# Scatter-add in two column halves into two output tensors, with GpSimd's weight copies moved to VectorE and ScalarE

## What is computed

```python
ys = _geglu(xf @ Ws1 + bs1) @ Ws2 + bs2              # shared expert, every token
top_val, top_idx = jax.lax.top_k((xf @ Wr + br) / TAU, 2)
top_w = jax.nn.softmax(top_val, axis=-1)             # w: its one-hot sum over 12 experts
h = jnp.einsum('nd,edh->enh', xf, We1) + be1[:, None, :]
act = _geglu(h)                                      # a * gelu(g), 768 wide
yE = jnp.einsum('enh,ehd->end', act, We2) + be2[:, None, :]
yr = jnp.einsum('end,ne->nd', yE, w)
x = x + (ys + yr)
```

## Time and profile before

| | us |
|---|---|
| median of 3 runs | 805.79 |
| profiled execution, its own time | 806.17 |
| its span | 804.4 |
| PE busy (share of the span) | 783.6 (97%) |
| DVE busy | 575.9 (72%) |
| ACT busy | 294.3 (37%) |
| POOL busy | 405.4 (50%) |
| 75 indirect scatters on POOL (L504) | 120.6 |
| 75 indirect gathers on POOL (L496) | 75.1 |
| POOL's 75 copies of a weight block and 75 of the bias part | 30.4 and 42.8 |

### The profile page before, as it was taken

One profiled execution on the slowest core, in us unless ns is written; L12 is line 12 of the kernel. 1 busy time (PEld: TensorE's weight loads), 2 busy tenths in 40 slices (PEclk: granted clock), 3 DMA queues, 4 the chain that ended last, 5 costly groups with the idle time before them and its releaser, 6 DMA issues.

```text
span 804.4 us, 27682 instructions
## 1 busy us (share of the span) xinstructions
PE 783.6 (97%) x9379; PEld 658.2 (82%) x9380; DVE 575.9 (72%) x1350; ACT 294.3 (37%) x883; POOL 405.4 (50%) x511
## 2 busy tenths in 40 slices
PE   7999999999999999999999999999999999999994
PEld 6788888888888888777778888888888888888883
DVE  2999877777777777679884676666666666666661
ACT  1444444444444444542222333333333333333330
POOL 3133244444444444401012777777777777777762
PEclk9999999999999999999999999999999999999998
DMA  9553355555565554048734233223222322232222
GB/s 277 153 187 101 112 170 180 182 174 177 180 182 181 182 182 146 2 158 232 231 130 139 28 42 37 33 35 39 35 34 33 38 38 33 34 40 36 33 31 26
DMA packets 49325, 86.11 MB, mean 107 GB/s; under 512 B 7298, under 2 KB 27970, under 8 KB 49122
## 3 DMA queue, kind: packets, MB, share of 16 engines
q1 hardware_dynamic: 33778, 68.83, 27.2%
q0 software_dynamic: 13888, 15.13, 14.3%
q10 hardware_dynamic: 1584, 1.10, 0.5%
HBM read 68.48 MB, written 16.55 MB: 106 GB/s over the span
## 4 chain that ended last, share of the span: by engine, by line
PE 90%; DVE 5%; issue 2%; DMA 1%; SPq 0%; POOL 0%; ACT 0%; DVEq 0%
PE ps L1575 24%; PE ps L1562 13%; PE ps L1234 7%; PE ps L1473 6%; PE ps L1332 4%; PE ps L1556 4%; PE ps L1306 3%; PE ps L1250 3%; PE ps L1279 3%; PE ps L1462 3%; PE ps L1219 3%; PE ps L1543 2%; PE ps L1339 2%; PE ps L1292 2%; PE ps L1321 2%
## 5 line engine op out<-in xcount | busy, mean ns | idle before, releaser
L1575 PE MATMUL ps<-arena,stage 128*128 x900 | 206.6, 379 | 0.0
L1575 PEld LDWEIGHTS ps<-arena,stage 128*128 128x128 f32 x900 | 165.2, 190 | 19.5
L504 POOL DMA_INDIRECT out_dram<-stage,to_row x75 | 120.6, 1609 | 76.0 <-DVE stage L1143 71.3
L708 ACT ACTIVATE stage<-ps 128x384 f32<-128x384 f32 x150 | 65.4, 488 | 241.6 <-PE ps L1562 241.6
L1562 PE MATMUL ps<-token_rows,token_rows_T 64*128 64x128 f32 x1800 | 129.2, 272 | 0.0
L1562 PEld LDWEIGHTS ps<-token_rows,token_rows_T 64*128 64x128 f32 x1800 | 118.8, 188 | 1.7
L496 POOL DMA_INDIRECT token_rows<-gated_rows,from_row x75 | 75.1, 1001 | 61.6 <-DVE to_row L1022 38.9
L1117 DVE COPY token_rows<-ps 128x128 f32<-128x128 f32 x75 | 21.9, 292 | 111.8 <-PE ps L1544 111.8
L408 POOL TENSOR_TENSOR arena<-arena 128x256 f32<-128x256 f32 x32 | 23.4, 732 | 139.3 <-DVE arena L832 132.3
L1127 DVE TENSOR_TENSOR stage<-ps,stage 128x384 f32<-128x384 f32 x150 | 76.0, 549 | 1.8 <-ACT stage L708 1.8
L795 DVE TENSOR_REDUCE arena<-ps 128x8 f32<-128x512 f32 x64 | 43.9, 686 | 42.4 <-PE ps L1270 42.0
(11 more groups left out here) (173 smaller groups left out, 1473.8 us busy)
## 6 DMA issues: line engine op xcount, KB each, us to landing
stage<-in_we_dram SPq DMA_DIRECT2D x36, 512.0 KB, 4.7
arena<-in_cond_w_dram SPq DMA_DIRECT2D x64, 256.0 KB, 2.8
arena<-in_we_dram SPq DMA_DIRECT2D x12, 768.0 KB, 6.0
arena<-in_x_both_dram SPq DMA_DIRECT2D x31, 256.0 KB, 2.7
arena<-in_L_cond_bias_dram SPq DMA_DIRECT2D x64, 64.0 KB, 2.9
out_dram<-arena SPq DMA_DIRECT2D x32, 128.0 KB, 2.7
be_bc<-in_be_rows_dram SPq DMA_DIRECT2D x13, 192.0 KB, 3.4
gated_rows<-token_rows POOLq DMA_DIRECT2D x2, 1152.0 KB, 11.6
```

What stands on the lines that cost most here:

```text
L504: pool.indirect_dma_start(out_rows, bass.IndirectOffsetOnAxis(to_row[:, t:t + 1], 0), y_sb[t % YR], None, compute_op=ALU.add).then_inc(d_a ...
L708: nc.scalar.activation(g_sb[hf].rearrange("p (j n) -> p j n", n=P), first_out[1][:, :, hf, :], ACT.Gelu).then_inc(g_ok, 1)
L1575: last = mm(ps[:, 4 + s % 2, 0:D], actT_sb[s % 2][:, hf, j * P:(j + 1) * P], arena[:, ds(e * E2 + (NJ * hf + j) * D, D)], start=(hf == 0 a ...
```

## The change

Each scatter is made in two halves of 128 columns, into two output tensors of 128 columns, which are put side by side on the host. Each half has a semaphore of its own and waits for the same half of the tile before. The stores of the shared expert and the padding rows are split in the same way: two DMAs each for one. POOL's `copy_last` is gone, and its waits with it. DVE copies block 2 besides block 1, with a load of `expert_of` for each; ACT copies the bias part besides block 0, in a new function `tile_weights`.

```diff
-        d_add = sem("d_add")
+        d_add = [sem(f"d_add{h}") for h in range(2)]
...
                 sp.wait_ge(comb_ok, n + 1)
-                sp.dma_start(out_rows[ds(n * P, P), :], x2res[:, ds(n * D, D)]).then_inc(d_out, 16)
+                for h in range(2):
+                    sp.dma_start(out_half[h][ds(n * P, P), :], x2res[:, ds(n * D + h * P, P)]).then_inc(d_out, 16)
...
             def add_rows(t, s):
                 pool.wait_ge(y_ok, t + 1)
-                if t > 0:
-                    pool.wait_ge(d_add, 16 * t)
-                pool.wait_ge(d_dummy, 16)
-                pool.indirect_dma_start(out_rows,
-                                        bass.IndirectOffsetOnAxis(to_row[:, t:t + 1], 0),
-                                        y_sb[t % YR], None, compute_op=ALU.add).then_inc(d_add, 16)
-
-            def copy_last(t):
-                copy_first(pool, nc.gpsimd.tensor_copy, t, t, 2)
-                e = pool.value_load(expert_of[0:1, ds(t, 1)], min_val=0, max_val=NE - 1)
-                nc.gpsimd.tensor_copy(w1bx[t % 2].bitcast(bf16), w1b[:, ds(e * (NJ * P), NJ * P)]).then_inc(w1bx_ok, 1)
+                pool.wait_ge(d_dummy, 32)
+                for h in range(2):
+                    part = slice(h * P, (h + 1) * P)
+                    if t > 0:
+                        pool.wait_ge(d_add[h], 16 * t)
+                    pool.indirect_dma_start(out_half[h],
+                                            bass.IndirectOffsetOnAxis(to_row[:, t:t + 1], 0),
+                                            y_sb[t % YR][:, part], None, compute_op=ALU.add).then_inc(d_add[h], 16)
...
-            pool.wait_ge(r_done, 1)
-            pool.wait_ge(shx_ok, TOK // U)
-            pool.wait_ge(l_cut, 4 * (NE + 1))
-            for t in range(2):
-                copy_last(t)
...
             for t in range(NS):
-                if t + 2 < NS:
-                    pool.wait_ge(h_ps, t + 1)
-                    copy_last(t + 2)
                 if t > 0:
                     add_rows(t - 1, (t - 1) % RING)
...
+            def tile_weights(t, s):
+                copy_first(act, copy, t, s, 0)
+                e = act.value_load(expert_of[0:1, ds(t, 1)], min_val=0, max_val=NE - 1)
+                copy(w1bx[s % 2].bitcast(bf16), w1b[:, ds(e * (NJ * P), NJ * P)]).then_inc(w1bx_ok, 1)
...
                     if s + 2 < left:
-                        copy_first(act, copy, t + 2, s, 0)
+                        tile_weights(t + 2, s)
                         widen(t + 2, (s + 2) % RING, 16 * q + (16 if s + 2 < RING else 32))
...
                 if not (isinstance(t, int) and t < YR):
-                    dve.wait_ge(d_add, 16 * t - 16 * (YR - 1))
+                    for h in range(2):
+                        dve.wait_ge(d_add[h], 16 * t - 16 * (YR - 1))
...
                     if not last or s + 2 < NS % RING:
-                        copy_first(dve, V.tensor_copy, t + 2, s, 1)
+                        for j in (1, 2):
+                            copy_first(dve, V.tensor_copy, t + 2, s, j)
                     gate_bias(t, s)
```

More of the change, by code:

```diff
@@ L40, with adaln_attn_moe @@
 ALI = P + 4 * S
-def adaln_attn_moe(nc, args, out):
+def adaln_attn_moe(nc, args, out_half):
     f32, bf16, i32, u32 = mybir.dt.float32, mybir.dt.bfloat16, mybir.dt.int32, mybir.dt.uint32
@@ L47, in adaln_attn_moe @@
     a = args
-    out_rows = out
     ctx = ExitStack()
@@ L380, in _ @@
                     store_out(2 * u + v, d_out_low)
-            sp.wait_ge(d_out_low, 16 * low_tiles)
+            sp.wait_ge(d_out_low, 32 * low_tiles)
             for e in overlap:
@@ L454, in _ @@
             pool.dma_start(gated_rows[PAD_ROW:PAD_ROW + P, :], zero_row).then_inc(d_zero, 16)
-            pool.dma_start(out_rows[TOK:TOK + P, :], zero_out).then_inc(d_dummy, 16)
+            for h in range(2):
+                pool.dma_start(out_half[h][TOK:TOK + P, :], zero_out[:, 0:P]).then_inc(d_dummy, 16)
             def tile_steps(i, odd, last=False):
@@ L516, in _ @@
                 load_rows(s, s)
-            pool.wait_ge(r_done, 1)
-            pool.wait_ge(shx_ok, TOK // U)
-            pool.wait_ge(l_cut, 4 * (NE + 1))
-            for t in range(2):
-                copy_last(t)
-            pool.wait_ge(d_out_low, 16 * low_tiles)
-            pool.wait_ge(d_out_high, 16 * (NT - low_tiles))
+            pool.wait_ge(d_out_low, 32 * low_tiles)
+            pool.wait_ge(d_out_high, 32 * (NT - low_tiles))
             for t in range(NS):
-                if t + 2 < NS:
-                    pool.wait_ge(h_ps, t + 1)
-                    copy_last(t + 2)
                 if t > 0:
@@ L532, in _ @@
             add_rows(NS - 1, (NS - 1) % RING)
-            pool.wait_ge(d_add, 16 * NS)
+            for h in range(2):
+                pool.wait_ge(d_add[h], 16 * NS)
         @block.scalar
@@ L722, in _ @@
             act.wait_ge(shx_ok, TOK // U)
+            act.wait_ge(l_cut, 4 * (NE + 1))
             for t in range(2):
@@ L725, in _ @@
             for t in range(2):
-                copy_first(act, copy, t, t, 0)
+                tile_weights(t, t)
             shared_gelu(TOK // U - 1)
@@ L1064, in _ @@
             dve.wait_ge(d_zero, 16)
-            dve.wait_ge(d_dummy, 16)
+            dve.wait_ge(d_dummy, 32)
             dve.wait_ge(l_cut, 4 * (NE + 1))
@@ L1166, in _ @@
             for t in range(2):
-                copy_first(dve, V.tensor_copy, t, t, 1)
+                for j in (1, 2):
+                    copy_first(dve, V.tensor_copy, t, t, j)
             for v in range(2):
@@ L1705 @@
                                     kind="ExternalInput").ap()
-    out = nc.dram_tensor("out_0_dram", (TOK + P, D), mybir.dt.float32, kind="ExternalOutput").ap()
-    adaln_attn_moe(nc, args, out)
+    out_half = [nc.dram_tensor(f"out_{h}_dram", (TOK + P, P), mybir.dt.float32, kind="ExternalOutput").ap()
+                for h in range(2)]
+    adaln_attn_moe(nc, args, out_half)
     r = run_bass_kernel_spmd(nc, [arrays], core_ids=[0])
-    return r.results[0]["out_0_dram"][:TOK].reshape(B, S, D)
+    return np.concatenate([r.results[0][f"out_{h}_dram"][:TOK] for h in range(2)], axis=1).reshape(B, S, D)
```

## The result

The changed kernel takes 829.93 us, median of 4 runs (829.41 to 830.89), against 805.9 before: a ratio of 1.0301, 95% interval 1.0288 to 1.0314. The profiled execution took 829.45 us.

A forecast was written before the change was run, and what follows sets the result against it. PE at 4.73 us a tile bounds the kernel before; the change makes POOL the bound at 5.21. From 445.85, 69 x 5.21 plus the tail gives span 834.8, 836 against the median; range 808 to 860.

The forecast's parts named there:

- the chain of landings: Waits between scatters: landing 3.8 us plus 0.7 to the next start allows one per 4.5 us, under PE's 4.73.
- Half a scatter at full price: On POOL, each half scatter costs 1.61 us like a whole, as the rows stay 128 and both halves still add.
- Three gaps of 0.307: On POOL, one gap for each of three indirect DMAs a tile, 0.92 us together.
- busy time alone: POOL's period without the gaps, 4.22 us, which would fit under PE's 4.73.
- 0.07 a tile for the port: POOL loses 0.07 us a tile to DVE's copies and bias multiply, which get through mostly in the gaps.
- The way from POOL to PE: A slow POOL reaches PE through DVE's y, which waits for landings; PE idle 0.4 to 0.5 us a tile.
- The five last steps: Tail without gathers: the chain of landings sets 4.2 us a step, with a half landing after 3.5.
- Copies on VectorE and ScalarE, stores in halves, PE's clock: Load of the moved copies on DVE and ACT, 32 more store issues, and a lower PE clock: no cost expected.
- A price by bytes: Rival: POOL's half scatter costs 1.19 us, PE keeps 4.73, no loss, time 805; chance 0.16.
- The port as a dear term: Rival: port sharing between DVE and POOL makes 5.5 to over 6 us a tile, 890 at 6.0; chance 0.10.
- The Trainium skill's fit: DMA time as 2.0 us + bytes / 436e3: a half lands only 0.15 sooner, the sum 1 us higher.
- The argument from transfers under 64 KB: Against the scatter split: the skill's rule that transfers under 64 KB mostly pay overhead; no size given.

The follow-up runs named there:

- e1: Kernel before with only the copies moved from POOL to DVE and ACT, the scatter left whole: 805.71 us against 805.89.
- e7: e1 with one more gather a tile, into a buffer that nothing reads: 806.73 us.
- e4: The changed kernel with half scatters that write instead of adding: 803.21 us, one execution.
- e10: e1 with its whole scatter writing instead of adding: 801.93 us, one execution.
- e3: The changed kernel with each half scatter cut to the first 64 of its 128 rows: 809.06 us, a single execution.
- e8: e1 with two more gathers a tile, into buffers that nothing reads: 879.04 us.
- e6: The changed kernel with block 2 copied by ScalarE and not by VectorE: 829.66 us against the change's 829.93.
- e2: The changed kernel with the scatter split but the copies left on POOL: 883.62 us, ratio 1.0963 to the kernel before.

## Why the prediction was right, and where it was off

- **What bounds the kernel before**: PE at 4.73, with the chain of landings at 4.5 and POOL's three instructions under it. Right; e1 and e7 change POOL's load in both directions and the time stays. That loosening the chain buys nothing is right too: e4 brings it from 4.5 down to 2.9 us, and the pace stays 4.73.
- **Half a scatter at full price**: taken 1.61, measured 1.58. The reason given, that the adding and not the bytes makes the price, is shown by e4 and e10. The other half of it, "since the number of rows stays 128", hardly counts: 64 rows cost 1.43 (e3).
- **Three gaps of 0.307**: right (0.305), and shown by e8 to be time that POOL can't use: without them it would have kept PE's pace. The 4.22 of "busy time alone" would have said that the change is free.
- **0.07 a tile for the port**: wrong. The step that failed reads: "a DVE copy from SBUF to SBUF waits for POOL's indirect DMA. POOL will be in one for nearly all of the period, so the two copies and the bias multiply get through mostly in the gaps". They don't need the gaps, as DVE's and POOL's timelines show together:

```profile
603.04 1.02 POOL L497 DMA_INDIRECT token_rows<-gated_rows,from_row  x1 [0.30 <-issue]
...
603.58 0.28 DVE L269 COPY token_rows_T<-w_merged 128x256 f32 x1
...
604.37 1.58 POOL L507 DMA_INDIRECT out_dram<-stage,to_row  x1 [0.31 <-issue]
...
604.87 0.68 DVE L1131 TENSOR_SCALAR token_rows_T<-be_bc,token_rows 128x256 f32 x1 [0.48 <-issue]
```

The copy lies wholly inside a gather and takes 0.28, as when POOL does nothing. The multiply inside the scatter is held up, to 605.55, 0.40 before the scatter's end and not after it. POOL did not lose 0.07 a tile but about 1 us in all 75: 24 of the 150 halves took longer than 1.58, by 1.1 us together. Taking one of the three operations away (e6) changed nothing. The step rested on one row beside a POOL copy, in which a VectorE copy that begins 0.34 into a gather is held to its end. In e1, where no POOL copy follows the gather, copies that begin up to 0.53 into it take about 0.29.
- **The way from POOL to PE**: wrong as well, at no cost to the sum. The prediction has PE "waiting for DVE's y, which itself waits for landings". The runs show the gathers in that place: ACT waits for gathered rows in 35 of 40 tiles, 65.8 us in 200, and DVE's sum for no landing. PE's tile is 0.36 us longer, 5.09 for 4.73, near the "PE idle 0.4 to 0.5 a tile" of the forecast, though the busy column doesn't show it.
- **The size.** The span came to 827.1 where my sum had 834.8. Of the 7.7 us, 8.1 come from the period, 69 x 5.21 = 359.5 against 351.3: 0.07 for the port, 0.06 for two halves at 1.58 and not 1.61, less 0.02 for a longer gather. The five last steps took 4.02 and not 4.2 (0.9), the last landing 3.3 and not 3.5 (0.2). Against that the stage began 0.3 later, and the program's close behind the last landing took 4.4 and not 3.1. Without the charge for the port the sum would have come to 830.0. The longer close was not foreseen; by luck it hides 1.3 us of what the sum had too much.
- **Copies on VectorE and ScalarE, stores in halves, PE's clock**: no cost foreseen. None was found for the copies (e1) and the clock (1.00 in the stretch). No run splits the stores alone; at most they hold the 0.3 us by which the first scatter came later.
- **Rivals.** A price by bytes is out (e10). The port as a dear term is out by the 1.1 us above, VectorE's load by e1 and e6.
- The Trainium skill's fit, DMA: Bandwidth & Descriptors, "Anatomy of one DMA", would let a half land 0.15 sooner; the landing came 0.5 sooner (3.3 for 3.8), so here the measurement stands. For scatters that don't add it is near the fit, 2.2 for 2.4 (e4, e10). The same section calls descriptor generation small; POOL's instruction for one indirect DMA takes 1.0 to 1.6 us here, and is the bound.
- The argument from transfers under 64 KB doesn't reach this split: a half holds 64 KB, not less, and in e4 the same halves, not adding, cost nothing.

## What to carry to other kernels

Count an indirect DMA on POOL by its instruction time plus the gap of 0.3 us behind it, and compare that sum, not the busy time, with the pace of the engine that bounds. Splitting an adding scatter halves neither: POOL pays the price again for each piece. Before loosening a chain of waits, compare its step (landing plus 0.7) with the pace it would have to beat. Where one queue holds scatters and gathers, look for the effect of slow scatters in late gathers too; here it was there, and not in the y buffers.

## What the runs showed beyond that

- POOL's time for an indirect DMA of 128 rows is 0.94 to 1.02 us for a gather or a plain scatter, whether the rows have 288, 512 or 1024 bytes, and mostly 1.55 to 1.62 for one that adds; with 64 rows, 1.43 (e3). The adding costs landing time too: 3.3 against 2.2 for a half (e4).
- DVE's copy and bias multiply are held up only by a part of POOL's indirect DMA. In the changed kernel's trace, operations that begin 0.50 to 0.81 into an adding scatter end 0.40 before its end; those that begin in the first 0.4 run freely; in a gather those that begin up to 0.59 are free, and from 0.61 to 0.78 they end 0.09 after it. In the kernel before, one that began 0.34 into a gather was held to its end. There a POOL copy is next in the queue, here and in e1 another indirect DMA; e1 points to that copy as the cause, and no run tries it alone.
- The holding up goes the other way too. The Trainium skill, SBUF — State Buffer, "SBUF: two separate sides", gives the shared port pair to whichever of the two starts first, and has a GpSimd DMA wait for DVE. Of the 24 longer scatters, 19 had one of these DVE operations still running 0.13 to 0.24 into them, and ended 1.43 to 1.46 after it; the longest, in which a DVE copy had begun 0.05 before it, took 1.69 for 1.58. Both agree with the page, save that neither holds for the whole instruction.
- The gap ahead of an indirect DMA depends on what stands before it: 0.30 behind another indirect DMA, 0.16 behind a copy (e2).
- The close of the program after the last landing took 4.4 us in the changed kernel and 3.1 before. The difference lies in POOL's last instruction, a DRAIN: 2.68 us before and 2.69 in e1, 3.87 in the change and e2, 4.20 in e7, 6.07 in e3, 7.26 in e8. It goes neither by the number of DMAs alone (e4 has 150 scatters and 2.77, e10 has 75 and 3.99) nor by the span, and what sets it stays open. A difference of a few us between two kernels can lie there.
